# A cross-attention and mixture-of-experts kernel: folded weights laid out by batch, expert weights loaded during attention, shared rows stored into the second accumulator, 22 tiles routed early

## The reference

```python
x = x + xattn(layernorm(x), context)      # 16 heads of 64, 64 keys a batch
x = x + ffn(layernorm(x))

# ffn, with E = 8 experts, two chosen per row, hidden width H = 352
scores = softmax(xf @ gate_w.T)           # (T, 8)
_, idx = top_k(scores + gate_b, 2)        # choice with a bias, weights without
rw = scores at idx, zero elsewhere
h  = silu((xf @ w1[e] + b1[e]) * (xf @ w3[e] + b3[e]))
oe = h @ w2[e] + b2[e]
y  = sum_e rw[:, e] * oe                  # only the two chosen experts count
z  = the same expert form with the shared weights sw1, sw3, sw2
return x + y + z
```

## Time and profile before

| | |
|---|---|
| median of 3 runs | 782.56 us (779.53 to 783.23) |
| profiled execution | 776.01 us, span of its instructions 774.3 us |
| mean granted TensorE clock | 0.955 of full speed |
| busy share of the span | PE 88%, DVE 70%, POOL 53%, ACT 51% |
| data moved | 80.09 MB, mean 103 GB/s |

### The profile page before, as it was taken

The page is one execution under the profiler, slowest core; times in us unless marked ns, Lnnn a source line. Parts: engine busy times, 40 slices in busy tenths (PEclk is TensorE's granted clock), DMA queues, the critical chain, the costliest instruction groups (busy, mean ns, idle before and its releaser), DMA issues.

```text
span 774.3 us, 16857 instructions
## 1 busy us (share of the span) xinstructions
PE 680.5 (88%) x4645; PEld 635.6 (82%) x4646; DVE 538.7 (70%) x1105; ACT 397.5 (51%) x1291; POOL 406.7 (53%) x505
## 2 busy tenths in 40 slices
PE   4996899999899899758478369999999999999995
PEld 3784699989888799647477269999999999999994
DVE  4974788878888877468388256666666666666678
ACT  3984787777676767326332113443443443434432
POOL 5443565454487777623234503777677677676300
PEclk9997999999999999968799779999999999999998
DMA  8202343222223322279763132555544444445495
GB/s 235 77 1 72 124 150 90 80 73 69 58 72 62 71 57 55 62 231 310 197 113 63 25 99 51 77 78 70 76 73 70 78 68 72 77 88 103 93 393 222
DMA packets 75109, 80.09 MB, mean 103 GB/s; under 512 B 21530, under 2 KB 67972, under 8 KB 75044
## 3 DMA queue, kind: packets, MB, share of 16 engines
q1 hardware_dynamic: 57700, 55.76, 26.3%
q0 software_dynamic: 15760, 18.96, 15.2%
q10 hardware_dynamic: 1584, 4.59, 1.5%
HBM read 49.84 MB, written 29.43 MB: 102 GB/s over the span
## 4 chain that ended last, share of the span: by engine, by line
PE 73%; DMA 13%; DVE 7%; issue 3%; POOL 2%; SPq 1%; ACT 1%; ACTq 0%; POOLq 0%; DVEq 0%
PE ps L1184 61%; DMA slots_scratch<-record,slot 12%; PE ps L1361 4%; PE ps L1281 3%; PE ps L1353 2%; PE ps L1258 1%; POOL slots_scratch L647 1%; DMA wq_sb<-in_L_xattn_Wq 1%; PE ps L1271 1%; DVE hmax L977 1%; PE ps L1308 1%; SPq L526 0%; DVE sums L1117 0%; SPq L525 0%; DVE prob L982 0%
## 5 line engine op out<-in xcount | busy, mean ns | idle before, releaser
L697 POOL DMA_INDIRECT acc_scratch<-yrow,slots x71 | 112.1, 1579 | 85.7 <-ACT yrow L866 85.3
L866 ACT ACTIVATE yrow<-ps,slots 128x256 f32<-128x256 f32 x71 | 33.7, 474 | 148.1 <-PE ps L1184 133.4
L647 POOL DMA_INDIRECT slots_scratch<-record,slot x64 | 64.8, 1013 | 79.4 <-DMA slots_scratch<-record,slot 62.7
L1184 PE MATMUL ps<-w13h,uxTh 128*128 x284 | 97.6, 344 | 0.0
L1103 DVE TENSOR_TENSOR uv<-ps,b 128x704 f32<-128x704 f32 x71 | 63.3, 891 | 47.5 <-PE ps L1184 45.4
L1184 PE MATMUL ps<-w13h,uxTl 128*128 x284 | 91.6, 322 | 0.0
L1184 PE MATMUL ps<-w13l,uxTh 128*128 x284 | 91.3, 322 | 0.0
L876 ACT ACTIVATE uxTh<-ps 128x256 fp32r<-128x256 f32 x103 | 38.9, 378 | 93.4 <-PE ps L1353 64.3
L690 POOL DMA_INDIRECT xrow<-xn_scratch,slots x71 | 69.8, 983 | 25.7 <-issue 20.7
L755 ACT ACTIVATE prob<-ps,nmax 128x64 f32<-128x64 f32 x256 | 76.4, 338 | 2.2 <-DVE nmax L980 2.2
L1184 PE MATMUL ps<-Uh,pTh 128*128 128x256 f32 x256 | 74.7, 292 | 0.0
(11 more groups left out here) (241 smaller groups left out, 2171.7 us busy)
## 6 DMA issues: line engine op xcount, KB each, us to landing
sums<-acc_scratch SPq DMA_DIRECT2D x16, 512.0 KB, 10.3
w_raw<-in_L_ffn_w SPq DMA_DIRECT2D x16, 352.0 KB
xin<-in_x SPq DMA_DIRECT2D x32, 128.0 KB
acc_scratch<-yrow ACTq DMA_DIRECT2D x8, 512.0 KB, 2.6
xres<-in_x SPq DMA_DIRECT2D x32, 128.0 KB
acc_scratch<-x SPq DMA_DIRECT2D x32, 128.0 KB
xn_scratch<-xn SPq DMA_DIRECT2D x32, 128.0 KB
xrow<-xn_scratch SPq DMA_DIRECT2D x32, 128.0 KB
```

What stands on the lines that cost most here:

```text
L647: pool.indirect_dma_start(slots_dram, bass.IndirectOffsetOnAxis(ap=slot[:, k, t:t + 1], axis=0), record[:, t, k, :], None).then_inc(scat_o ...
L697: pool.indirect_dma_start(acc_dram[u % 2], bass.IndirectOffsetOnAxis(ap=slots[:, u, 0:1], axis=0), yrow[:, m % YRING, :], None, compute_op ...
L866: act.activation(yrow[:, y, :], ps[:, 6 + m % 2, 0:D], ACT.Copy, scale=slots[:, bass.ds(u, 1), 1].bitcast(F32)).then_inc(y_ok, 1)
L1184: last = pe.matmul(out, stationary(k, a), moving(k, b), start=(k == 0 and i == 0), stop=(k == n - 1 and i == len(PARTS) - 1 and not more))
```

## The change

- `NA` becomes 16 and `NB` 16: 16 shared tiles ahead of the routed units and 16 behind them.
- A third group of six tiles, (16, 22), is routed during attention; REST are 10 tiles. POOL's record scatters follow a schedule of one tile a step up to step 31 and two tiles a step in steps 32 to 36 (`scattered_by`).
- A and U lie in one tensor `AU` by batch, 32 KB a partition and batch, so that a batch's part is free when its eight tiles are done. `w13_raw` and `w2_raw` lie over it from the start. SP loads w1 and w3 of experts 0 to 4 in steps 13 to 17, of 5 to 7 in steps 21 to 23, w2 of experts 0 to 5 in steps 24 to 29, of 6 and 7 in steps 31 and 32.
- The high parts of w1 and w3 of experts 0 to 4 are made by ACT in steps 31 to 35 of attention, the low parts by DVE in steps 33 to 37; the rest is made in the first unit steps (w2 high in 1 to 4, w1/w3 high in 5 to 7, w2 low in 4 to 11, w1/w3 low in 12 to 14).
- The first 8 x rows of the shared units are loaded in step 20 of attention.
- A shared tile's result is copied by ACT into yrow and stored by ACT's DMA queue into the second accumulator, without x2 and without DVE. The second accumulator's zeros are stored for the last 16 tiles alone.
- SP has only `shared_x` ahead of its wait for the records, and all 71 `unit_slots` behind it.

The diff, cut to its core:

```diff
+    EARLY13, EARLY2 = 5, 6
...
-    NA = 20
+    NA = 16
     NB = NT - NA
     R0, R1 = NA, NA + NU
-    GROUPS = ((0, 8), (8, 16))
-    REST = (16, NT)
-    NREST = NT - 16
+    GROUPS = ((0, 8), (8, 16), (16, 22))
+    REST = (22, NT)
+    NREST = NT - 22
     STAGES = 6
...
+        AU = sb("AU", [P, B, 4, KD * HK], F32R, att)
+        Ah, Al = (AU[:, :, i, :].rearrange("p b (k n) -> p b k n", k=KD) for i in (0, 1))
+        Uh, Ul = (AU[:, :, i, :].rearrange("p b (j d) -> p b j d", j=NJ) for i in (2, 3))
...
+            def load_w13(e):
+                sp.wait_ge(O_ok, TPB if e < EARLY13 else 2 * TPB)
+                sp.dma_start(w13_raw[:, e, :, 0:H], w1[e, :, :].rearrange("(k p) h -> p k h", p=P)).then_inc(raw13_in[e], 16)
+                sp.dma_start(w13_raw[:, e, :, H:2 * H], w3[e, :, :].rearrange("(k p) h -> p k h", p=P)).then_inc(raw13_in[e], 16)
+
+            def load_w2(e):
+                sp.wait_ge(pad2_zero, 1 if e < EARLY2 else 2)
+                sp.dma_start(w2_raw[:, e, 0:KH - 1, :], w2[e, 0:(KH - 1) * P, :].rearrange("(c p) d -> p c d", p=P)).then_inc(raw2_in[e], 16)
+                sp.dma_start(w2_raw[0:HR, e, KH - 1, :], w2[e, (KH - 1) * P:H, :]).then_inc(raw2_in[e], 16)
+                sp.dma_start(w2_raw[HR:HR + 1, e, KH - 1, :], b2[e, :].rearrange("(a d) -> a d", a=1)).then_inc(raw2_in[e], 16)
+
+            def begin_step(s, par):
+                tile_step(s, par)
+                if s in (13, 14, 15, 16, 17):
+                    load_w13(s - 13)
+                if s in (21, 22, 23):
+                    load_w13(s - 16)
+                if 24 <= s < 24 + EARLY2:
+                    load_w2(s - 24)
+                if s in (31, 32):
+                    load_w2(s - 25)
+                if s == 20:
+                    for half in xn2_out:
+                        sp.wait_ge(half, 16 * RING // 2)
+                    for t in range(RING):
+                        shared_x(t)
 
             def shared_x(t):
...
             def shared_x(t):
                 m, i = t % RING, shared_tile(t)
                 wait(sp, X_ok, t - RING + 1)
                 sp.dma_start(xrow[:, m, :], xn2_tiles[:, i // TPB, i % TPB, :]).then_inc(xrow_in[m], 16)
...
-            def shared_x2(t):
-                m = t % YRING
-                wait(sp, sum_row_out[m], 16 * (t // YRING))
-                sp.dma_start(yrow[:, m, :], acc_tiles[0][:, t // TPB, t % TPB, :]).then_inc(x2_in[m], 16)
-
-            def shared_sum(t):
-                m = t % YRING
-                sp.wait_ge(sum_row_ok, t + 1)
-                sp.dma_start(acc_tiles[0][:, t // TPB, t % TPB, :], yrow[:, m, :]).then_inc(sum_row_out[m], 16)
+            steps(NT, 3, 5, begin_step, begun=0)
...
+            for t in range(RING, NA):
+                shared_x(t)
+            sp.wait_ge(eid_ok, 1)
+            for half in scat_out:
+                sp.wait_ge(half, 16 * NT)
+            for u in range(NU):
                 unit_slots(u)
...
+            def scattered_by(step):
+
+                done = 0
+                for s in range(step + 1):
+                    routed = max([b for _, b in GROUPS if b + 6 + STAGES <= s], default=0)
+                    done = min(routed, done + (1 if s < NT else 2))
+                return done
+
...
-                for g, (a, b) in enumerate(GROUPS):
-                    t = a + s - (b + 6 + STAGES)
-                    if a <= t < b:
-                        pool.wait_ge(slot_ok, g + 1)
-                        for k in range(TOP):
-                            scatter_record(t, k)
+                for t in range(scattered_by(s - 1), scattered_by(s)):
+                    pool.wait_ge(slot_ok, 1 + [t < b for a, b in GROUPS].index(True))
+                    for k in range(TOP):
+                        scatter_record(t, k)
+                if s == 22:
+                    pool.wait_ge(O_ok, 2 * TPB)
+                    pool.memset(w2_raw[:, 0:EARLY2, KH - 1, :], 0.0).then_inc(pad2_zero, 1)
+                if s == 30:
+                    pool.wait_ge(O_ok, 3 * TPB)
...
+                if 31 <= s < 31 + EARLY13:
+                    high13(s - 31)
...
+                if s < NB // QUAD:
+                    b, j = divmod(NA + s * QUAD, TPB)
+                    zero_rows(acc_tiles[1][:, b, j:j + QUAD, :])
+                if 8 <= s < 11:
+                    zero_rows((acc_dram[0], xn2_dram, acc_dram[1])[s - 8][T:T + PADS, :].unsqueeze(1))
...
+            def high13(e):
+                act.wait_ge(raw13_in[e], 32)
+                if e < EARLY13:
+                    act.wait_ge(O_ok, 3 * TPB)
...
+            def high2(e):
+                act.wait_ge(raw2_in[e], 48)
                 flat = [a[:, e, :, :].rearrange("p c d -> p (c d)") for a in (w2h, w2_raw)]
-                act.activation(flat[0], flat[1], ACT.Copy).then_inc(w_hi, 1)
...
+            def shared_z(t):
+                act.wait_ge(shared_row_ok, t + 1)
+                act.dma_start(acc_tiles[1][:, t // TPB, t % TPB, :], yrow[:, t % YRING, :]).then_inc(shared_row_out[t % YRING], 16)
...
+                    elif t < R0:
+                        wait(act, Y_ok, t + 1)
+                        wait(act, shared_row_out[y], 16 * (t // YRING))
+                        act.activation(yrow[:, y, :], ps[:, 6 + m % 2, 0:D], ACT.Copy).then_inc(shared_row_ok, 1)
...
+                if isinstance(s, int) and 1 <= s < 1 + E // 2:
+                    high2(2 * s - 2)
+                    high2(2 * s - 1)
+                if isinstance(s, int) and 5 <= s < 5 + E - EARLY13:
+                    high13(s - 5 + EARLY13)
...
+                if 33 <= s < 33 + EARLY13:
+                    low13(s - 33)
+
+            def low13(e):
+                for k in range(KD):
+                    wait(dve, w13_hi, KD * e + k + 1)
+                    last = dve.tensor_tensor(w13l[:, e, k, :], w13_raw[:, e, k, :], f32(w13h[:, e, k, :]), ALU.subtract)
+                last.then_inc(w_lo, 1)
+
+            def low2(e):
+                wait(dve, w2_hi, e + 1)
+                flat = [a[:, e, :, :].rearrange("p c d -> p (c d)") for a in (w2l, w2_raw, w2h)]
+                dve.tensor_tensor(flat[0], flat[1], f32(flat[2]), ALU.subtract).then_inc(w_lo, 1)
...
-                if is_shared(t, routed) and t < R0:
-                    p, y = m % 2, m % YRING
-                    wait(dve, Y_ok, t + 1)
-                    wait(dve, x2_in[y], 16 * (t // YRING) + 16)
-                    dve.tensor_tensor(yrow[:, y, :], ps[:, 6 + p, 0:D], yrow[:, y, :], ALU.add).then_inc(sum_row_ok, 1)
...
+                if isinstance(s, int) and 4 <= s < 4 + E:
+                    low2(s - 4)
+                if isinstance(s, int) and 4 + E <= s < 4 + E + E - EARLY13:
+                    low13(s - 4 - E + EARLY13)
...
-                        pe.wait_ge(xTl_ok, s + 1)
+                        pe.wait_ge(xTl_ok, min(s + 1, NT))
+                        pe.wait_ge(lg_ok, s - 5)
```

More of the change, by code:

```diff
@@ L387, in is_routed @@
             return R0 <= t < R1 if isinstance(t, int) else routed
-        def is_shared(t, routed):
-            return has(t, NALL) and not is_routed(t, routed)
         def shared_tile(t):
@@ L1066, in begin_step @@
                     if 0 <= stage < STAGES:
-                        route(stage, g, a, b, marked[:, :, :, :], mark[:, :, :, :], score[:, :, :], biased[:, :, :],
-                              chosen[:, :, :], gv[:, :, :], rank[:, :, :])
+                        n = b - a
+                        if stage == 0 and n < 8:
+                            link(dve.memset(chosen[:, n, :], 0.0))
+                        route(stage, g, a, b, marked[:, :, 0:n, :], mark[:, :, 0:n, :], score[:, 0:n, :], biased[:, 0:n, :],
+                              chosen[:, :, :], gv[:, :, 0:n], rank[:, :, :])
+                if 33 <= s < 33 + EARLY13:
+                    low13(s - 33)
+            def low13(e):
+                for k in range(KD):
+                    wait(dve, w13_hi, KD * e + k + 1)
[5 more added lines that the diff above has]
+                dve.tensor_tensor(flat[0], flat[1], f32(flat[2]), ALU.subtract).then_inc(w_lo, 1)
             dve.wait_ge(small_in, 80)
@@ L1337, in unit_step @@
                     elif t < R0 + 2:
[L1338 removed]
+                        wait(pe, shared_row_ok, t - 1)
                     else:
```

118 lines of the change are left out of this document (36 added, 82 removed).

## The result

The changed kernel takes 760.94 us (median of 4 runs, 756.62 to 763.92) against 782.89 for the kernel before beside it (4 runs, 779.53 to 783.47): a ratio of 0.9724, 95% interval 0.9669 to 0.9779. It is faster by 2.8%; the forecast was 762. Its profiled execution took 756.62 us, span 754.9, clock 0.958; the span is 19.4 us shorter than before's 774.3. It was the fastest of the four, which lie 7.3 us apart.

The account below looks back on a forecast made before the run. PE was taken as full except in the transition, where x2 loads, x rows and records held it; 4.5 + 16.6 + 0.4 - 43.3 + 1.2 = -20.6 us from 782.6 gave 762, range 745 to 777.

Parts of the forecast that it names:

- (d): End of attention, tile 12's record to tile 31's layernorm: two tiles of records a step make it 37.8 us, +16.6.
- (e): Last router logits to unit 3: a low part adds 1.7, routing fewer tiles saves 1.3, together +0.4 us.
- (f): Unit 3 to unit 21: 68.1 us instead of 111.4, -43.3, with the late records hidden by 4 us to spare.
- (a): Shared rows: x2 loads and DVE additions go, ACT's copies and stores lie in its idle time; no separate size.
- (b): Weight loads moved into attention: 0 for the loads, 1.0 us for POOL's memset, 0.5 for ACT's high parts.
- The 7.41 a step: Sign for (b): scores and outputs staying at 7.41 us a step through attention steps 13 to 27.
- Rival 3: Weight loads slow attention, 16 loading steps each late by 2.7 us: 43 us on top, 805; chance 0.07.
- (c): Third early group routed in attention steps 28 to 33: 3.0 us; with (b) attention is late by 4.5.
- Rival 1: The tail of attention is short, (d) at its lower end of +5.6: 751 us; chance 0.15.
- (g): From unit 21 to the end: a second addition for quad 4 on a full DVE, +1.2 us.
- Rival 2: Records stay the bound, late tiles at 8.02 us each: 783, chance 0.05; half of it: 772, chance 0.10.
- Rival 4: DVE's low parts hold the shared units, (f) gives back 11 us more: 773; chance 0.03.

Follow-up runs that it names:

- run 7: Kernel before with the shared rows of its 20 tiles copied and stored by ACT, no x2 loads or DVE additions, else unchanged: 759.54 us, ratio 0.9751.
- run 11: run 7 plus four record scatters under way, x rows 8 to 12 between the weight loads, one low part a unit: 742.65 us, ratio 0.9522.
- run 10: run 9 with DVE's five low parts of steps 33 to 37 made in unit steps 12 to 16 instead: 740.27 us, ratio 0.951.
- run 9: Changed kernel with two early groups, 20 shared tiles ahead of the routed units and four record scatters under way: 740.31 us, ratio 0.9529.
- run 1: Changed kernel itself, unchanged, profiled again: 758.64 us, ratio 0.9737.
- run 2: Changed kernel with one tile of records scattered a step to the end of attention, the rest behind it: 763.81 us, ratio 0.9799.
- run 3: Changed kernel with four record scatters under way instead of two: 754.78 us, ratio 0.9682.
- run 8: Changed kernel without the third early group and two tiles of records a step, 20 shared tiles ahead of the routed units: 757.73 us, ratio 0.9757.
- run 12: Changed kernel with 20 shared tiles ahead of the routed units and four record scatters under way, third group kept: 744.47 us, ratio 0.9627.
- run 4: Changed kernel with the eight x rows loaded one a step instead of all at step 20: 762.57 us, ratio 0.9815.
- run 6: Kernel before with A and U side by side in one tensor by batch, nothing loaded earlier: 777.78 us, ratio 0.9989.

## Why the prediction was right, and what it missed

The mechanism holds: the transition's hole closed, and its price was paid at the end of attention. That the sum came out within 1.2 us is in part luck: attention was 5.7 us later than the sum has it, and (d), (e) and (f) gave 4.7 back. In the second profile of the same kernel (f) alone is 4.2 us longer.

**(a) Shared rows.** Costed at nothing on the path, which holds (PE waits for no yrow in the units). But the prediction gave the gain of (f) to the parts together and never asked what (a) brings alone. Run 7 says: as much as the whole change. The rest of the change then takes another 30 us out of the units (95.4 to 65.7) and puts 20.6 into attention (335.6 to 356.2). By ratio the two come out even; the single spans (761.3 and 754.9) say less, since the one was the slowest of its four executions and the other the fastest. Whether it was the x2 loads behind SP's wait, DVE's additions or both that cost the time, run 7 doesn't separate; the 17.27 us in front of 449.76 speak for the loads.

**(b) Weights.** Right that their loads cost nothing in their place: the five scalings from 166.78 to 198.83, beside the first five loads, are 7.52, 8.82, 7.67 and 8.04 us apart, before 7.52, 8.83, 7.67 and 8.05; and from 240.03 to 290.13, beside six more, are 50.1 us where before has 50.2. (The 7.41 a step that the prediction named as its sign holds in neither kernel for all of these steps; routing makes some longer in both.) Rival 3 is out. The 0.5 for ACT's high parts was probably too little. Where only tiles 12 to 15 are scattered ahead of the last layernorm, the last scaling to the last layernorm takes 328.4 - 312.5 = 15.9 us before and 14.9 in run 11, 19.3 in run 10 with the high parts alone, 20.8 in run 9 with the low ones too. Of the 3.4 between before and run 10, ACT's high parts and the pairing of tiles 12 to 15 were not separated.

**(c) The step that was mis-sized** is "attention is late by 4.5": it was 10.2. Three things are in it. What the prediction priced at 4.5 (third group 3.0, POOL's memset 1.0, high parts 0.5) comes to 10.2 - 4.5 - 2.6 = 3.1. The other 7.1 it had at nothing. The eight x rows of step 20, which the prediction named and did not price, are 2.6: the scalings of 230.07 and 240.03 lie 9.96 apart, the same two before 7.40. The cause is in SP's queue and DVE's wait, time lines of the changed kernel:

```profile
221.88 5.12 SPq L516 DMA_DIRECT2D xrow<-xn_scratch  x8
227.05 0.43 SPq L445 DMA_DIRECT2D xin<-in_x  x1
```

```profile
233.41 0.43 DVE L996 BATCH_NORM_STATS2 st<-xin 128x6 f32<-128x256 f32 x1 [3.69 <-DMA xin<-in_x]
```

The load of x stands behind 5.12 us of issuing. The price isn't fixed: this step and the next take 17.5 us together in run 1, 18.5 in run 9, 18.6 in the changed kernel's first profile and 20.1 to 20.4 in runs 2, 3, 8, 10 and 12, where before has 16.2. In run 3 the granted clock behind the wait was 0.64 and 0.51 (240 to 242 and 242 to 244 us), in the changed kernel it stayed at 1.00. The last 4.5 were there before attention began (first scaling at 79.79 for 75.30): the half clock at 43 to 53 us. The prediction read the lower level as what follows PE's idling; here PE had been idle for only 0.57 us in all from 20 to 43 us. It isn't tied to any one part. It shows in eight profiles (the changed kernel twice, runs 2, 3, 4, 8, 10 and 11; in run 4 at 41 to 51 us, in run 11 at 45 to 52) and not in six (before twice, runs 6, 7, 9 and 12). Run 9 has the whole layout and the early weights and runs at the full clock, run 11 has neither and does not. Why one build falls into it and another doesn't stays open, and so does whether a build always does: each of the two kernels profiled twice showed the same both times. (Runs 6 and 7 have the upper level there and still begin 2.6 and 2.7 us later than before, with their first scalings at 77.92 and 77.99; that wasn't followed up.)

**(d) Two tiles of records a step.** Predicted +16.6, measured +14.6: 4.43 us a tile where 4.7 was taken. Run 2 confirms that it is records (one tile a step gives 10.2 back) and run 3 that it is their landing (5.9 back). Rival 1, the short tail, is out. The Trainium skill (DMA: Bandwidth & Descriptors, Anatomy of one DMA) has a fixed cost of some 2.0 us for such a DMA. These chains show more than twice that, 4.43 us from a tile's record to the next tile's, which waits for it to land.

**(e)** and **(g)** came out within 0.3 us.

**(f) The units.** 65.7 for a predicted 68.1 (69.9 in run 1). The late records start at 367.32 (predicted unit 3 - 11.6 = 366.0), tile 31's at 411.23, nine intervals of 4.88 against 9 x 4.7 + 4.0; the first gather is at unit 3 + 41.7, predicted + 41.4. PE doesn't wait for it: it comes to unit 16 at unit 3 + 46.0, where + 48.7 was predicted, since the units themselves were quicker, and about 1 us was to spare instead of 4. In run 1, with the gather at + 36.8, it was more. Rival 2 was thus near, and run 2 shows its price: 10.9 us of PE for a gather 18.4 us later. Rival 4 is out for the changed kernel: units 5 to 12 follow each other at 3.54 us beside the low parts of w2, and the three of w1 and w3 cost 0.2 to 0.7 us each. It is real where both low parts of an expert fall into one unit (run 7).

**What (b) to (d) should have been.** The third group is not needed once four scatters are under way and 20 shared tiles cover them: run 9 without it has no wait for the gather, and run 12 with it is not faster. Four scatters alone, with three groups and 16 tiles, bring 4 us by median, within the intervals; with two groups and 20 tiles they remove the 7.1 us that PE waited for the first gather (run 9 against 8). Runs 9, 10 and 11 reach 740 to 743 us, 5% under before and 2% under the changed kernel, on two routes: fill the units with early weights and keep attention short (9), or leave attention nearly as it was and treat the three waits of the units (11).

## What to carry to other kernels

Before costing a change of many parts as one sum, ask what the first part is worth alone: here the shared rows' way out was as much as all of the gain, and the rest moved 20 to 30 us from one place to another. Look at the stretches that a comparison takes for equal, too: two versions that start attention within 0.4 us of each other can lie 4.5 us apart by step 24, with stretches at the lower clock in one of them alone (runs 9 and 12). Work moved ahead of a boundary is paid at the boundary if the engine that does it also carries the last link (POOL's layernorm behind its own scatters). Where a chain waits for landings, put more of it under way before moving it; and price each DMA issue of a moved step, since the next load stands behind it.

## What the runs showed of the hardware

- PE's granted clock fell to the lower level for some 10 us (43 to 53 us) in preparation while PE was busy 6.00 of 6.00 us at 44 to 50; from 36 to 40 us it had been busy 3.43 of 4. The change alters where the results of the preparation lie, not its products. The first scaling came 4.5 us later, against the whole change's gain of 19.4, and this can turn up between two versions that are being compared.
- A chain of record scatters (two a tile, 128 entries of 8 bytes each, each waiting for that of the tile before) took 4.43 us a tile at the end of the changed kernel's attention and 8.02 in the transition of the kernel before, while loads ran at 264 GB/s, though POOL is busy with a tile for only 2 x 0.96 us.
- POOL's operations on one column took 0.74, 1.08 and 1.22 us beside a DVE subtraction of two on-chip inputs and 0.19, 0.55 and 0.26 without it; an indirect scatter took 1.56 for 0.96. The Trainium skill's rule (SBUF — State Buffer, Who interferes with whom) agrees. Moving the low parts away made the way from the last scaling to the last layernorm 1.5 us shorter (run 10 against 9). In both POOL stood waiting for DVE's statistics before that layernorm (2.31 and 3.10 us).
